# Attention and feed-forward in one kernel: scores in batches of two, the last sum of tiles 0 to 6 turned through DRAM, and tanh operations behind the exps

## The chip, the cores and the metric

One core of a Trainium2 chip runs the whole kernel. The metric is device time in microseconds (us) of one execution: the median of three runs. A core has TensorE (PE, matrix products), ScalarE (ACT), VectorE (DVE), GpSimd (POOL) and SyncE (SP, which only issues transfers here). Each takes its own instructions strictly in order and waits on semaphores for the others.

## What is computed

`x` has 4096 tokens of 256 channels. First attention with 16 heads of 16 channels, then a feed-forward part with three blocks, each inside a layer norm and with a residual:

```
x = x + LN(attention(LN(x)))                   # causal softmax, 16 heads; q, k, v and proj with low-rank terms
x = x + LN(ffn(LN(x)))
ffn: h = x
     for blk in 0, 1, 2:
         y = W[2 blk] h + b;  y = gelu(LN(y) * gamma + beta)
         h = h + W[2 blk + 1] y + b            # six 256 x 256 weights, dequantised, with low-rank terms
```

## The kernel before

A first stage loads and folds weights, projects q, k and v, and writes q and k to DRAM. The rest, which is what the change touches, is `attend_and_feed`. Tokens are cut in 8 tiles of 512. Attention walks through 32 visits (a tile's queries, four heads each). For each block of 128 keys and pair of heads it makes one *score unit*: two products of 64 rows into one of three slots `S` of PSUM (`NS = 3`), then one exp of 128x1024 by ScalarE into `probs`, a ring of twelve. A *weigh* multiplies four heads' `probs` with the values into the one bank `O`: four products on 128x32 strips of the array, of 512 columns each (fewer on the diagonal). At the end of a visit VectorE turns `O`, divides, and SP moves the result to `attT`. There are 1056 score units and 576 weighs.

Meanwhile the *feed* works on tiles whose attention is complete: the output projection, layer norms and the three blocks. Tiles 0 to 6 are fed as 14 halves of 256 tokens in three lanes of buffers, the last tile in four parts after the last exp. A feed *piece* is the product of four strips of 256 columns into the one bank `F`. A half's sum `h` is held with channels on partitions; layer norms want tokens on partitions. In between, a half is turned by a VectorE transpose of 32x32 blocks ("flip"), four transfers to DRAM ("put") and one back ("get"). The last product of the third block, `second2` (called `ENDING`), is made the other way round, with tokens on partitions, so that its result can be normalised where it is; for that TensorE also adds `h` by products with the identity (the branch `c == NC` in the printed function), and `evac_h` on VectorE adds the bias.

What stands where is not decided while it runs. `plan()` walks through the whole stage with durations of its own and writes down an order for each engine; the engines run these orders as they stand. In `plan()`, `next_product` chooses TensorE's next item: a batch of scores goes on while it has fewer than `BATCH` and the next slot is free within `THIRD` us; feed pieces become due at `FEED_FROM + FEED_EACH * tile`; `BACKLOG` is the number of units that weighs may lag. Going over from scores (64 rows) to strips (32 columns) and back is a *turn* below. ScalarE's own list has exps and, for tiles 0 to 6, 42 tanh operations of 128x512 (`gelu0` to `gelu2` of 14 halves), taken ahead of any exp that is ready at the same time.

Of the kernel before, what the change touches and what calls it, by code (L numbers as in the profile page):

```python
# [23 lines left out]
P = 128  # L24
# [9 lines left out]
STRIP = 32  # L34
# [787 lines left out]
FEED_FROM, FEED_EACH = 24.0, 62.0  # L822
BATCH, THIRD, SLACK, BACKLOG = 3, 0.25, 0.5, 10
HOP = 0.15
LANDING = {"k_load": 4.3, "q_load": 4.3, "moved": 1.9, "x_load": 4.2, "store": 3.0, "moved_late": 1.9}
TURNS = ["_x"] + [str(m) for m in range(BLK)]
# [75 lines left out]
def feed_parts():  # L902

    parts = [("evac_att", 0.8, 0.45, ("project",)), ("ln_att", 1.75, 1.05, ("evac_att",)), ("rs_att", 1.9, 1.9, ("ln_att",)),
             ("add_x", 1.5, 1.1, ("rs_att", "x_load")), ("ln_x", 1.75, 1.05, ("add_x",)), ("rs_x", 1.9, 1.9, ("ln_x",)),
             ("norm_x", 0.95, 0.6, ("rs_x",)), ("flip_x", 0.75, 0.0, ("norm_x",)), ("put_x", 2.8, 0.0, ("flip_x",)), ("get_x", 0.7, 0.0, ("put_x",))]
    for m in range(BLK):  # L910
# [38 lines left out]
def plan():  # L949
# [41 lines left out]
    for x in feed:  # L991
# [85 lines left out]
    def next_product(now):  # L1077
# [10 lines left out]
        slack = busy - (now + HOP + us[score] + SWITCH["score"]) if first else 1e9  # L1088
# [21 lines left out]

    locked, F_free, blocked = None, 0.0, {}
# [5 lines left out]
    while len(end) < len(after):  # L1117
# [36 lines left out]
def attend_and_feed(nc, g, d):  # L1154
# [26 lines left out]
    with ExitStack() as ctx:  # L1181
# [124 lines left out]
        with nc.Block() as block:  # L1306

            @block.sync
            def _(sp):
                need = sp.value_load(g["need_max"][0:1, 0:1], min_val=0, max_val=1)  # L1310
                for x in order["SP"]:
# [145 lines left out]
            def _(pe):  # L1457
# [47 lines left out]
                for x in order["PE"]:  # L1505
# [46 lines left out]
                    elif name.startswith("second") and name != ENDING:  # L1552
# [28 lines left out]
            def _(dve):  # L1581
# [64 lines left out]
                for x in order["DVE"]:  # L1646
# [39 lines left out]
                    elif name.startswith("flip"):  # L1686
                        nc.vector.transpose(flat[2][s][:, :], flat[3][s][:, :]).then_inc(dve_ok[s], 1)
# [19 lines left out]
                    elif name.startswith("add") and m is not None:  # L1707
                        for o in range(NC):
                            last = nc.vector.scalar_tensor_tensor(own_t(hT, t, k)[:, o, :], in_channels(name, t, k)[:, o, :],  # L1709
                                                                  g["b2T"][:, m * NC + o:m * NC + o + 1], own_t(hT, t, k)[:, o, :], ALU.add, ALU.add)  # L1710
# [25 lines left out]
                    else:  # L1736
                        link(s, scaled(t, k, own(u, t, k)))
# [55 lines left out]
```

## Time and profile before

| | us |
|---|---|
| median of three runs | 1263.21 (1259.63 to 1264.57) |
| the profiled execution's own time | 1261.49 |
| its span, first to last instruction | 1259.5 |
| PE busy in the span | 1213.4 |
| ACT busy in the span | 1097.8 |
| DVE busy in the span | 754.9 |

Busy time is the union of an engine's instructions. Matmul ends are modelled and two neighbours overlap, so what a product costs is read from the distance between the starts of groups, not from its length. Idle time counts only where the engine is the one that sets the pace.

### The profile page before, as it was taken

To read this page: it belongs to the slowest core of one execution; us is meant where nothing else is said; L and a number is where in the kernel's file an instruction comes from. 1 tells how busy PE (TensorE), PEld (TensorE's weight loads), DVE (VectorE), ACT (ScalarE), POOL (GpSimd) and SP (SyncE) were. 2 spreads that over 40 slices of the span, in tenths; PEclk is the share of its full clock that TensorE was granted. 3 is DMA by queue.
4 is the path that set the end of the run, shared out by engine and by line. 5 is a ranking of instruction groups with operands and counts; after the bars stand their busy time and mean duration, and the time that the engine had idled before them with its cause. 6 is when DMAs were issued, how large, how long until landed. Compare 5 with 4: busy or idle time off the path is not lost.

```text
span 1259.5 us, 30041 instructions
## 1 busy us (share of the span) xinstructions
PE 1213.4 (96%) x11429; PEld 526.9 (42%) x11429; DVE 754.9 (60%) x1820; ACT 1097.8 (87%) x1251; POOL 437.9 (35%) x1373
## 2 busy tenths in 40 slices
PE   8999999999999999999999999999999999999957
PEld 6556434343343433444334334343344333333246
DVE  6775225577765666766665675756666665551066
ACT  4765999999999998999999999999899999999922
POOL 3221235343433552345334253432323431220044
PEclk9999999999999999999999999999999999999989
DMA  5985644644435453454443443543435343331000
GB/s 170 314 307 174 191 122 119 187 150 132 140 102 151 123 143 86 126 164 135 123 122 102 122 119 107 137 118 107 137 86 158 110 129 102 89 93 47 1 5 17
DMA packets 144208, 159.48 MB, mean 127 GB/s; under 512 B 76326, under 2 KB 106044, under 8 KB 144060
## 3 DMA queue, kind: packets, MB, share of 16 engines
q1 hardware_dynamic: 139772, 153.26, 41.0%
q10 hardware_dynamic: 4288, 4.26, 1.1%
q8 instruction: 91, 1.49, 0.5%
q14 instruction: 57, 0.47, 0.1%
HBM read 117.62 MB, written 35.65 MB: 122 GB/s over the span
## 4 chain that ended last, share of the span: by engine, by line
PE 68%; ACT 7%; DVE 5%; issue 3%; DMA 3%; POOL 2%; SPq 2%; ACTq 0%; POOLq 0%; DVEq 0%
PE O L1500 30%; PE S L1482 21%; PE F L209 15%; ACT probs L1425 6%; SPq L595 2%; DMA feed_mem<-turns 2%; DMA qkv_mem<-turns 1%; DVE feed_mem L1703 1%; PE S L1571 1%; DVE feed_mem L1704 1%; DVE o_turned L1652 1%; PE S L1555 0%; POOL rstdC L1385 0%; DVE stC L1594 0%; DVE feed_mem L1727 0%
## 5 line engine op out<-in xcount | busy, mean ns | idle before, releaser
L1425 ACT ACTIVATE probs<-S 128x1024 f32<-128x1024 f32 x1056 | 995.2, 1050 | 65.1 <-PE S L1482 56.1
L1500 PE MATMUL O<-probs,vg 128*32 128x512 f32 (+3 forms) x4608 | 523.9, 564 | 5.3 <-DVE o_turned L1652 3.4
L1482 PE MATMUL S<-q_op,k_op 64*128 64x512 f32 (+3 forms) x2304 | 383.9, 425 | 9.9 <-ACT probs L1425 8.2
L1482 PEld LDWEIGHTS S<-q_op,k_op 64*128 64x128 f32 x2304 | 186.5, 184 | 324.2 <-ACT probs L1425 235.3
L1500 PEld LDWEIGHTS O<-probs,vg 128*32 128x32 f32 x4608 | 120.7, 110 | 208.6 <-issue 177.8
L1403 POOL TENSOR_SCALAR_AFFINE_SELECT probs<-probs 128x512 f32<-128x512 f32 (+1 forms) x160 | 92.9, 590 | 164.6 <-ACT probs L1425 164.0
L1373 POOL TENSOR_SCALAR tmpC<-mvC 128x2 f32<-128x2 f32 x84 | 24.4, 290 | 309.3 <-DVE rstdC L1603 307.4
L209 PE MATMUL F<-wfT,feed_mem 128*32 128x256 f32 x1280 | 83.5, 388 | 3.1 <-DVEq L1637 1.5
L1652 DVE STREAM_TRANSPOSE o_turned<-O 128x512 f32<-128x512 f32 x32 | 22.8, 712 | 97.1 <-PE O L1500 96.1
L1704 DVE SCALAR_TENSOR_TENSOR feed_mem<-feed_mem 128x512 f32<-128x512 f32 x90 | 65.9, 732 | 3.1
L1703 DVE SCALAR_TENSOR_TENSOR feed_mem<-feed_mem 128x512 f32<-128x512 f32 x90 | 63.6, 707 | 3.5 <-DVE qkv_mem L1709 0.5
L1412 POOL TENSOR_TENSOR feed_mem<-feed_mem 128x512 f32<-128x512 f32 x30 | 33.3, 1109 | 91.7 <-DVE feed_mem L1692 91.7
L560 PE MATMUL psQ<-xnT,qkv_mem 128*128 128x512 f32 x128 | 57.1, 599 | 1.7 <-POOL heads_of L449 1.7
L1685 DVE TENSOR_TENSOR feed_mem<-F,bffn 128x512 f32<-128x512 f32 x40 | 27.6, 689 | 50.4 <-PE F L209 50.4
L209 PEld LDWEIGHTS F<-wfT,feed_mem 128*32 128x32 f32 x1280 | 39.2, 111 | 44.3 <-issue 24.9
L1727 DVE TENSOR_SCALAR feed_mem<-feed_mem,rstdC,nmrC 128x256 f32<-128x256 f32 x80 | 34.6, 474 | 36.6 <-POOL nmrC L1384 35.5
L1594 DVE BATCH_NORM_STATS2 stC<-feed_mem 128x6 f32<-128x256 f32 x132 | 49.5, 416 | 10.1 <-DVEq L1637 7.6
L423 ACT ACTIVATE qf<-psQ,cols 128x512 f32<-128x512 f32 x32 | 21.9, 684 | 33.5 <-PE psQ L560 33.5
L1692 DVE TENSOR_SCALAR feed_mem<-feed_mem,halved 128x256 f32<-128x256 f32 x60 | 22.0, 409 | 36.1 <-DMA feed_mem<-turns 36.0
L1385 POOL TENSOR_TENSOR rstdC<-rstdC,minus_half 128x1 f32<-128x1 f32 x24 | 13.3, 554 | 80.2 <-DVE rstdC L1601 80.1
L209 PE MATMUL F<-feed_mem,wfT 128*32 128x256 f32 x640 | 40.9, 382 | 0.0
L560 PEld LDWEIGHTS psQ<-xnT,qkv_mem 128*128 128x128 f32 x128 | 23.7, 190 | 30.2 <-issue 28.3
(210 smaller groups left out, 1254.7 us busy)
## 6 DMA issues: line engine op xcount, KB each, us to landing
k_op<-qk_rows SPq DMA_DIRECT2D x256, 256.0 KB, 3.7
qk_rows<-parts SPq DMA_DIRECT2D x32, 512.0 KB, 4.4
q_op<-qk_rows SPq DMA_DIRECT2D x128, 128.0 KB, 2.9
turns<-feed_mem SPq DMA_DIRECT2D x160, 64.0 KB, 1.9
feed_mem<-turns SPq DMA_DIRECT2D x40, 256.0 KB, 2.9
k_op<-qk_rows SPq DMA_DIRECT2D x48, 128.0 KB, 2.6
x_in<-in_L_attn_x ACTq DMA_DIRECT2D x8, 512.0 KB, 5.3
feed_mem<-in_L_attn_x SPq DMA_DIRECT2D x16, 256.0 KB, 3.5
```

Of the source, the lines that this page charges most:

```text
L209: last = matmul(out[n * STRIP:(n + 1) * STRIP], lhsT[:, n, :] if len(lhsT.shape) == 3 else lhsT[:, n * STRIP:(n + 1) * STRIP], rhs, **how)
L560: last_mm = nc.tensor.matmul(psQ[:, m, :], g["wqkvT"][:, c, m * P:(m + 1) * P], xnT[:, u, c, :], start=(c == 0), stop=(c == NC - 1))
L1403: nc.gpsimd.affine_select(out=tri, in_=tri, compare_op=ALU.is_ge, fill=0.0, base=0, pattern=pattern, channel_multiplier=-1).then_inc(cut_o ...
L1412: nc.gpsimd.tensor_tensor(own_t(uT, t, k), z, z, ALU.mult).then_inc(pool_ok[lane(t, k)], 1)
L1425: nc.scalar.activation(probs[:, n % NP, :, :], S[:, n % NS, :, :], ACT.Exp, scale=SCALE).then_inc(exp_ok, 1)
L1482: last = nc.tensor.matmul(S[:, n % NS, a, at:at + TT - q0], k_op[mine, c % RING, pair, k0:k0 + P], q_op[mine, v % QS, pair, q0:TT], start= ...
L1500: last = nc.tensor.matmul(O[h * STRIP:(h + 1) * STRIP, q0:TT], vg[:, kb, col:col + STRIP], probs[:, n % NP, a, at:at + TT - q0], start=fir ...
L1594: last = nc.vector.bn_stats(st[:, b.start + j, :], src[:, j, :])
L1652: nc.vector.transpose(o_turned[:, :, :].rearrange("p b e -> p (b e)"), O[:, :]).then_inc(o_out, 1)
L1703: link(s, nc.vector.scalar_tensor_tensor(poly, poly, GELU_POLY[n], square, ALU.add, ALU.mult))
L1704: nc.vector.scalar_tensor_tensor(poly, poly, GELU_POLY[n - 1], by, ALU.add, ALU.mult).then_inc(dve_ok[s], 1)
L1727: last = nc.vector.tensor_scalar(flat[3][s].rearrange("p (i b r) -> p b i r", b=nb, r=STRIP)[:, j], src[:, j, :].rearrange("p (i r) -> p i ...
```

## The change

It has three parts, and with new numbers in `plan()` all orders of the stage come out anew. A batch holds at most two scores (`BATCH` 3 to 2, with smaller `THIRD` and `SLACK`), and two waits inside the plan get prices of their own (`SCORE_OUT`, `SLOT_OUT`). A tanh yields to an exp for 4 us after it is ready (`rank_now`). And for tiles 0 to 6 `second2` is made with channels on partitions like the other blocks' second products; `add2` on VectorE adds product, bias and `h` in four operations, and the half is turned by `flip_h`, `put_h` and `get_h` before its last layer norm. The two pieces per half that added `h` on TensorE go. The last tile keeps the old way.

```diff
-FEED_FROM, FEED_EACH = 24.0, 62.0
-BATCH, THIRD, SLACK, BACKLOG = 3, 0.25, 0.5, 10
+FEED_FROM, FEED_EACH = 20.0, 64.0
+BATCH, THIRD, SLACK, BACKLOG = 2, 0.2, 0.1, 11
 HOP = 0.15
+GELU_WAIT = 4.0
+SCORE_OUT, SLOT_OUT = 0.2, 0.15
-TURNS = ["_x"] + [str(m) for m in range(BLK)]
+TURNS = ["_x"] + [str(m) for m in range(BLK)] + ["_h"]
...
-    return 1 if name.startswith("turn") else nb * (NC + 1) if name == ENDING else nb * NC if name[:6] != "second" else NC * NC
+    return 1 if name.startswith("turn") else nb * NC if name[:6] != "second" else NC * NC
...
-    return parts + [("ln_h", 1.75, 1.05, ("evac_h",)), ("rs_h", 1.9, 1.9, ("ln_h",)), ("result", 1.5, 1.1, ("rs_h",)),
+    return parts + [("flip_h", 0.75, 0.0, (f"add{BLK - 1}",)), ("put_h", 2.8, 0.0, ("flip_h",)), ("get_h", 0.7, 0.0, ("put_h",)), ("ln_h", 1.75, 1.05, ("get_h",)), ("rs_h", 1.9, 1.9, ("ln_h",)), ("result", 1.5, 1.1, ("rs_h",)),
...
-        slack = busy - (now + HOP + us[score] + SWITCH["score"]) if first else 1e9
+        slack = busy - (now + SCORE_OUT + us[score] + SWITCH["score"]) if first else 1e9
...
+    def rank_now(x, now):
+
+
+        return 2 if x[0].startswith("gelu") and x[1] < NT - 1 and now < ready["ACT"][x] + GELU_WAIT else rank[x]
...
+                            if x[0] == "put_h":
+                                sp.dma_start(d["turns"][s].rearrange("(b r) (k q) -> r b k q", r=STRIP, q=NC * STRIP)[:, :, i, :],
+                                             flat[3][s][i * STRIP:(i + 1) * STRIP, :].rearrange("r (b q) -> r b q", q=NC * STRIP)).then_inc(put_ok[s], 16)
+                                continue
...
+                        if x[0] == "get_h":
+                            sp.dma_start(u[s], d["turns"][s].rearrange("(b p) n -> p b n", p=P)).then_inc(got_ok[s], 16)
+                            continue
...
-                    elif name.startswith("second") and name != ENDING:
+                    elif name.startswith("second") and (name != ENDING or t < NT - 1):
...
-                        nc.vector.transpose(flat[2][s][:, :], flat[3][s][:, :]).then_inc(dve_ok[s], 1)
+                        into, src = (3, 2) if name == "flip_h" else (2, 3)
+                        nc.vector.transpose(flat[into][s][:, :], flat[src][s][:, :]).then_inc(dve_ok[s], 1)
...
+                            into = flat[2][s].rearrange("p (b i c r) -> p c b i r", b=nb, c=NC, r=STRIP)[:, o]
+                            new, old = (x.rearrange("p (i b r) -> p b i r", b=nb, r=STRIP) for x in (new, old))
+                            for b in range(nb):
+                                last = nc.vector.scalar_tensor_tensor(into[:, b], new[:, b], by, old[:, b], ALU.add, ALU.add)
...
-                        link(s, scaled(t, k, own(u, t, k)))
+                        link(s, scaled(t, k, own(u, t, k), True))
```

How the order of TensorE moves is seen in the middle of the stage. Before, from score unit 477 on (L1482 is a score, two products each; L1500 a weigh, four each; L209 with `wfT` feed pieces, four each, and with `ident` the pieces that add `h`):

```order
L1482 MATMUL S<-q_op,k_op 128x512 x6
L1500 MATMUL O<-probs,vg 32x512 x4
L209 MATMUL F<-wfT,qkv_mem 32x256 x8
L209 MATMUL F<-ident,qkv_mem 32x128 x8
L1482 MATMUL S<-q_op,k_op 128x512 x6
L209 MATMUL F<-wfT,qkv_mem 32x256 x8
L209 MATMUL F<-ident,qkv_mem 32x128 x8
L1500 MATMUL O<-probs,vg 32x512 x4
L1482 MATMUL S<-q_op,k_op 128x512 x6
L1500 MATMUL O<-probs,vg 32x512 x8
L1482 MATMUL S<-q_op,k_op 128x512 x6
L1500 MATMUL O<-probs,vg 32x512 x8
```

With the change, from unit 482 on (the score is now L1499, the weigh L1517):

```order
L1499 MATMUL S<-q_op,k_op 128x512 x4
L1517 MATMUL O<-probs,vg 32x512 x8
L1499 MATMUL S<-q_op,k_op 128x512 x4
L1517 MATMUL O<-probs,vg 32x512 x4
L1499 MATMUL S<-q_op,k_op 128x512 x4
L1517 MATMUL O<-probs,vg 32x512 x8
L1499 MATMUL S<-q_op,k_op 128x512 x4
L1517 MATMUL O<-probs,vg 32x512 x4
L1499 MATMUL S<-q_op,k_op 128x512 x4
L1517 MATMUL O<-probs,vg 32x512 x8
L1499 MATMUL S<-q_op,k_op 128x512 x4
L209 MATMUL F<-qkv_mem,wfT 32x256 x8
```

Three scores and two weighs' worth of strips have become two scores with one and two weighs in turn. Over the whole stage the order has 371 turns there and back before the last score before, and 522 with the change.

On VectorE the end of the attention is the second place. Before (L1685 is `evac_h`, L1594 to L1603 moments, L1621 and L1738 the result, L1652 to L1663 turning and dividing `O`):

```order
L1685 TENSOR_TENSOR feed_mem<-F,bffn 128x512
L1594 BN_STATS stC<-feed_mem 128x6 x2
L1597 BN_AGGR mvC<-stC 128x2 x2
L1602 TENSOR_SCALAR tmpC<-mvC 128x2
L1603 TENSOR_SCALAR rstdC<-tmpC 128x2
L1621 TENSOR_SCALAR feed_mem<-feed_mem,rstdC,nmrC 128x256 x2
L1738 TENSOR_TENSOR feed_mem<-feed_mem 128x512
L1652 STREAM_TRANSPOSE o_turned<-O 128x512
```

With the change (L1741 is `add2`, L1711 the flip, L1611 to L1620 moments, L1675 to L1686 `O`, L1640 and L1769 the result):

```order
L1741 SCALAR_TENSOR_TENSOR feed_mem<-F,cols,feed_mem 128x4x32 x4
L1711 STREAM_TRANSPOSE feed_mem<-feed_mem 128x512
L1611 BN_STATS stC<-feed_mem 128x6 x2
L1614 BN_AGGR mvC<-stC 128x2 x2
L1619 TENSOR_SCALAR tmpC<-mvC 128x2
L1620 TENSOR_SCALAR rstdC<-tmpC 128x2
L1675 STREAM_TRANSPOSE o_turned<-O 128x512
L1680 RECIPROCAL o_rl<-o_turned 128x16
L1682 TENSOR_TENSOR o_turned<-o_turned,o_rl 128x16x16
L1686 STREAM_TRANSPOSE o_div<-o_turned 128x512
L1640 TENSOR_SCALAR feed_mem<-feed_mem,rstdC,nmrC 128x128 x4
L1769 TENSOR_TENSOR feed_mem<-feed_mem 128x512
```

The last half's moments, behind its flip and the transfers, now stand just ahead of the last turning of `O`, and its result behind it; before, the last half was done with one more visit still to come. In TensorE's order its last `second2` piece stands behind score unit 1044 of 1056, where it stood behind unit 985.

## Rows read from the trace of the kernel before

**Rows 1.** The page: busy time of each engine; the last chain by engine.

```profile
PE 1213.4 (96%) x11429; PEld 526.9 (42%) x11429; DVE 754.9 (60%) x1820; ACT 1097.8 (87%) x1251; POOL 437.9 (35%) x1373
PE 68%; ACT 7%; DVE 5%; issue 3%; DMA 3%; POOL 2%; SPq 2%; ACTq 0%; POOLq 0%; DVEq 0%
```

**Rows 2.** Windows: stretch, its length, PE, PEld, DVE, ACT, POOL busy, clock, DMA.

```profile
118.00:1196.00 1078.00, 1058.31 (x10732) 421.48 (x10732) 633.57 (x1436) 1013.48 (x1098) 384.77 (x1210) 1.00 0.42 120
```

**Rows 3.** One line's instructions: the scores (min/median/max ns; first and last start).

```profile
L1482 PE MATMUL S<-q_op,k_op x2304: 215/395/504, 118.0 to 1193.9; 64*128 64x512 f32 x160, 64*128 64x256 f32 x18, 64*128 64x128 f32 x14
```

**Rows 4.** Timeline of PE, 615.96 to 621.78 us, batches of three (start, length).

```profile
615.96 0.97 PE L1482 MATMUL S<-q_op,k_op 64*128 64x512 f32 x6
616.86 1.92 PE L1500 MATMUL O<-probs,vg 128*32 128x512 f32 x16
618.71 1.28 PE L1482 MATMUL S<-q_op,k_op 64*128 64x512 f32 x6
619.92 1.92 PE L1500 MATMUL O<-probs,vg 128*32 128x512 f32 x16
621.78 0.50 PE L1482 MATMUL S<-q_op,k_op 64*128 64x512 f32 x2
```

**Rows 5.** Timeline of PE, 216.34 to 217.99 us, batches of two.

```profile
216.34 0.73 PE L1482 MATMUL S<-q_op,k_op 64*128 64x512 f32 x4
217.00 1.07 PE L1500 MATMUL O<-probs,vg 128*32 128x512 f32 x8
217.99 0.73 PE L1482 MATMUL S<-q_op,k_op 64*128 64x512 f32 x4
```

**Rows 6.** The chain in order of time: two feed pieces.

```profile
591.08 0.86 PE F L209 x16
```

**Rows 7.** Timeline of ACT: exps back to back, and round a tanh (L1435).

```profile
1130.34 65.70 ACT L1425 ACTIVATE probs<-S 128x1024 f32<-128x1024 f32 x71 [0.34 <-PE S L1482]
...
600.87 0.64 ACT L1435 ACTIVATE qkv_mem<-qkv_mem 128x512 f32<-128x512 f32 x1
...
601.39 5.78 ACT L1425 ACTIVATE probs<-S 128x1024 f32<-128x1024 f32 x6
```

**Rows 8.** Timeline of PE, 1157.18 to 1159.02 us: batches of two, one weigh each.

```profile
1157.18 0.91 PE L1482 MATMUL S<-q_op,k_op 64*128 64x512 f32 x4
1158.02 1.07 PE L1500 MATMUL O<-probs,vg 128*32 128x512 f32 x8
1159.02 0.90 PE L1482 MATMUL S<-q_op,k_op 64*128 64x512 f32 x4
```

**Rows 9.** Timelines and a window round two longer stalls of PE.

```profile
484.81 3.60 PE L209 MATMUL F<-wfT,feed_mem 128*32 128x256 f32 x32 [1.54 <-DVEq L1637]
...
486.00:488.00 2.00, 2.00 (x24) 1.04 (x16) 1.90 (x4) 0.00 (x0) 0.00 (x0) 0.50 0.30 107
...
904.77 4.01 PE L1500 MATMUL O<-probs,vg 128*32 128x512 f32 x32 [1.99 <-DVE o_turned L1652]
```

**Rows 10.** Single lines of DVE: additions and flips (min/median/max ns).

```profile
L1709 DVE SCALAR_TENSOR_TENSOR feed_mem<-F,cols,feed_mem x42: 342/477/485, 269.0 to 1229.9; 128x256 f32<-128x256 f32 x40, 128x128 f32<-128x128 f32 x2
...
L1687 DVE STREAM_TRANSPOSE feed_mem<-feed_mem x40: 670/711/714, 206.7 to 1102.8; 128x512 f32<-128x512 f32 x40
```

**Rows 11.** DMA issues (KB, us to landing), one put, SP's waits (total, times, longest).

```profile
turns<-feed_mem SPq DMA_DIRECT2D x160, 64.0 KB, 1.9
feed_mem<-turns SPq DMA_DIRECT2D x40, 256.0 KB, 2.9
...
601.91 2.84 SPq L1343 DMA_DIRECT2D turns<-feed_mem  x4
...
SPq L1319 <- PE S L1482: 220.7, 48, 15.6
```

**Rows 12.** Waits of DVE for a root; timeline of DVE behind the last exp.

```profile
DVE feed_mem L1727 <- POOL nmrC L1384: 35.5, 23, 3.7
...
1203.13 0.43 DVE L1594 BATCH_NORM_STATS2 stC<-S 128x6 f32<-128x256 f32 x1 [3.69 <-PE S L1571]
```

More of the change, by code:

```diff
@@ L910, in feed_parts @@
     for m in range(BLK):
-        out = f"add{m}" if m < BLK - 1 else "evac_h"
         parts += [(f"evac{m}", 0.8, 0.45, (f"first{m}",)), (f"ln{m}", 1.75, 1.05, (f"evac{m}",)), (f"rs{m}", 1.9, 1.9, (f"ln{m}",)),
@@ L915, in feed_parts @@
                   (f"pa{m}", 1.45 + 0.45, 0.0, (f"sq{m}",)), (f"pb{m}", 1.45, 0.0, (f"pa{m}",)), (f"pc{m}", 1.45, 0.0, (f"pb{m}",)),
-                  (f"gate{m}", 0.75, 0.0, (f"gelu{m}",)), (out, 0.9, 0.55, (f"second{m}",))]
-    return parts + [("ln_h", 1.75, 1.05, ("evac_h",)), ("rs_h", 1.9, 1.9, ("ln_h",)), ("result", 1.5, 1.1, ("rs_h",)),
+                  (f"gate{m}", 0.75, 0.0, (f"gelu{m}",)), (f"add{m}", 0.9, 0.55, (f"second{m}",))]
+    return parts + [("flip_h", 0.75, 0.0, (f"add{BLK - 1}",)), ("put_h", 2.8, 0.0, ("flip_h",)), ("get_h", 0.7, 0.0, ("put_h",)), ("ln_h", 1.75, 1.05, ("get_h",)), ("rs_h", 1.9, 1.9, ("ln_h",)), ("result", 1.5, 1.1, ("rs_h",)),
                     ("store", 0.5, 0.5, ("result",))]
@@ L1004, in plan @@
             found += [("moved", 4 * t + i) for i in (0, 1, 2, 3) if n >= 1 + i // 2] + ([("moved_late", 4 * t + 3)] if n >= 2 else [])
-            found += [("exp", NUNIT - 1)] if k else [("evac_h", t - 1, j) for j in range(2)]
+            found += [("exp", NUNIT - 1)] if k else [(f"add{BLK - 1}", t - 1, j) for j in range(2)]
         if n == (lead(name) if t == NT - 1 else 0) and (t < NT - 1 or name != "project"):
@@ L1109, in landing, with hop @@
         return LANDING_FIRST if x[0] == "moved" and x[1] < FIRST_MOVED else LANDING.get(x[0], 0.0)
+    def hop(a, y):
+        return SCORE_OUT if y[0] == "exp" and a[0] == "score" else SLOT_OUT if y[0] == "score" and a[0] == "exp" else HOP
+    def rank_now(x, now):
+        return 2 if x[0].startswith("gelu") and x[1] < NT - 1 and now < ready["ACT"][x] + GELU_WAIT else rank[x]
     locked, F_free, blocked = None, 0.0, {}
@@ L1127, in plan @@
             start = now
-            x = min((x for x, at in ready[e].items() if at <= now), key=lambda x: (rank[x], -left.get(x, 0.0), ready[e][x], str(x)))
+            x = min((x for x, at in ready[e].items() if at <= now), key=lambda x: (rank_now(x, now), -left.get(x, 0.0), ready[e][x], str(x)))
         del ready[e][x]
@@ L1140, in plan @@
             if not waiting[y]:
-                ready[engine[y]][y] = max(end[a] + (0.0 if engine[a] == engine[y] and a[0] not in PUTS else 0.0 if not us[a] else landing(a) if engine[a] == "SP" or a[0] == "moved_late" else HOP) for a in after[y])
+                ready[engine[y]][y] = max(end[a] + (0.0 if engine[a] == engine[y] and a[0] not in PUTS else 0.0 if not us[a] else landing(a) if engine[a] == "SP" or a[0] == "moved_late" else hop(a, y)) for a in after[y])
                 if takes_bank(y):
@@ L1617, in root, with scaled @@
                     return nc.vector.scalar_tensor_tensor(nmr[:, b], mv[:, b, 0], -1.0, r, ALU.mult, ALU.mult)
-                def scaled(t, k, src):
+                def scaled(t, k, src, turned=False):
                     for j, b in enumerate(range(slots(t, k).start, slots(t, k).stop)):
+                        if turned:
+                            for c in range(NC):
+                                last = nc.vector.tensor_scalar(own(y, t, k)[:, j, :].rearrange("p (c k e) -> p c k e", c=NC, e=STRIP)[:, c],
+                                                               src[:, j, :].rearrange("p (k c e) -> p c k e", c=NC, e=STRIP)[:, c],
+                                                               rstd[:, b:b + 1], nmr[:, b:b + 1], ALU.mult, ALU.add)
+                            continue
                         last = nc.vector.tensor_scalar(own(y, t, k)[:, j, :], src[:, j, :], rstd[:, b:b + 1], nmr[:, b:b + 1], ALU.mult, ALU.add)
```

7 lines of the change are left out of this document (5 added, 2 removed).

## The prediction

> **What bounds the kernel now.** I read the page first: PE is busy 96% of the span and carries 68% of the last chain, ACT 87% and 7% [rows 1]. The stage that the change touches runs from the first score unit at 118.0 us to the last at 1193.9 us, 1075.9 us [rows 3]. In it PE is busy 1058 and ACT 1013 of 1078 us, DVE 634 [rows 2]. So two engines are nearly full, and each waits for the other. What PE's busy time hides is found from the starts of groups in its timeline. A batch of two scores takes 0.66 us until the weigh behind it starts, a weigh 0.99 us until the next score [rows 5]; two weighs take 1.85 us and three scores 0.90 us [rows 4]. The differences give 0.86 us for a weigh with 0.13 us on top once for a run of strips, and 0.22 us for a score unit (0.24 by the difference of 0.90 and 0.66; I take 0.22, since 0.66 = 2 x 0.22 + 0.22 and 0.90 = 3 x 0.22 + 0.24) with 0.22 on top once for a batch. One turn there and back so costs 0.35 us. Two feed pieces take 0.86 us [rows 6], so 0.43 each. An exp behind an exp takes 65.70 / 71 = 0.925 us, and a tanh holds the next exp up by 601.39 - 600.87 = 0.52 us [rows 7].
>
> PE's work in the stage: 1056 units x 0.22 = 234 (with three digits 0.222), weighs 453 (480 full ones x 0.858, and 32 of each narrower width, 1.5 x 32 x 0.858), feed pieces 189, and 371 turns x 0.35 = 130. That is 1006 us; PE stands still for the other 70. ACT's work is 1056 x 0.925 + 42 x 0.52 = 999. Neither sum explains 1076 alone. What does is the batch of three with three slots: its third score needs the slot of the unit just ahead of the batch, so PE waits for an exp that ACT can only end when it has nothing more to read. The batch at 615.96 takes 0.90 us, the next, with the same work, 1.21: 0.31 us of standing [rows 4]. If every other one of the 309 batches of three pays that, it is 48 us. Two long stalls are seen besides. At 484.81 PE waited 1.54 us for DVE, and its next four feed pieces took 3.60 in place of 1.72 us, at half the clock (granted share 0.50, so 1.2 GHz, right behind the wait); at 904.77 it waited 1.99 us for the turning of `O`, and four weighs took 4.01 where 3.5 was due [rows 9]. Together about 6 us. Towards the end of the stage, when the feed is through, batches of two with one weigh each come every 1.84 us: that is ACT's pace, and PE stands 0.84 - 0.66 = 0.18 us in each [rows 8]; the order has 28 of them in a row, 5 us. 48 + 6 + 5 leaves 11 us that I can't name.
>
> **The batches.** The order has 522 turns in place of 371: 151 x 0.35 = 53 us of PE work more. In return the third score's wait goes (-48). A batch of two needs slots whose exps ended one exp earlier. So what takes its place? The order gives each cycle (batch and strips behind it) one weigh in 226 cases, 0.35 + 0.44 + 0.86 = 1.65 us, 1.29 us of strips in 142 (2.08 us) and 1.72 in 117 (2.51 us); ACT wants 1.85. By a count 236 cycles are shorter than ACT's and 183 of these stand alone between longer ones. The rows at 216.34 show such a lone short cycle: no wait (0.66) [rows 5]. Those that follow another short one wait 0.18 as at 1157.18 [rows 8]: 236 - 198 (the runs' first ones) = 38, 7 us. It could be nothing if a long cycle ahead has given more play, and 0.18 x 236 = 42 if the lone ones wait as well; I take 7, because rows 5 are that case.
>
> A rule speaks against this part: the Trainium skill, TensorEngine Tiling (Array Packing), Key Properties, has it that a change of tiling mode drains TensorE. The skill's TensorE: Matmul & The Clock Gate puts what a lone matmul can't hide at about 166 ns at full clock. With two drains a turn that is an estimate of 0.33 us and +50 us for 151 turns; the trace's 0.35 agrees, and it has the rest of what a turn costs in it.
>
> **The tanh operations.** Before, one goes ahead of a ready exp, 0.52 us of ACT. Now 29 of 42 stand ahead of the first exp of a batch whose strips before were long (cycle 2.5 us or more, where ACT has 0.65 us free), 13 elsewhere. The first cost nothing, since ACT would wait for the score; the others at most 0.52 - 0.23 = 0.3 us (behind a 2.08 us cycle), together 3 us. A gain beyond that is none: ACT isn't the longer sum.
>
> **The last sum.** For each of 14 halves PE drops two pieces: 28 x 0.43 = -12 us, on the path, since PE has the longest sum. DVE drops `evac_h` (an operation of 128x512 like a flip, about 0.7) and makes four additions of 128x128 (0.34 each, the least of the line that has both forms) and a flip of 0.71 [rows 10], and the result in four operations in place of two, at worst 0.34 x 4 against two of 0.48, the median of a 128x256 there: 1.8 us a half, 25 in all on 634 of 1078, hidden while DVE is ahead of PE. SP issues 4 puts (2.84 us) and a get (0.6): 14 x 3.4 = 48 us of issuing. The half's way to its result grows by 1.4 + 0.7 - 0.7 + 2.8 + 1.9 + 0.6 + 2.9 = 9.6 us [rows 10, 11]. Nothing on PE waits for a result except the next half of the lane, whose place in the order is later by that. It costs nothing as long as DVE isn't held at `ln_h` with PE's inputs behind it; if it is, a case costs what those of rows 9 cost, 2.4 to 3.4 us.
>
> **The end.** The last `second2` piece is now 12 units ahead of the last exp, 11 us. From there addition 1.4, flip 0.7, put 4.7, get 3.5, moments 1.5 (two statistics of 0.43 and four short ones), the root on POOL at most 3.7 (the longest wait of DVE for one), result 2: 17.5 us, so the result ends 6.5 us behind the last exp. The last tile's moments start 7.1 us behind it (1203.13 against 1196.04), after 3.69 us in which DVE is idle, where the result fits [rows 7, 12]. Cost 0; each us beyond 0.6 is one on the time.
>
> **Sum.** PE's work: 1006 + 53 - 12 = 1047. Standing: 7 for short cycles, 3 for tanh, and 6 + 11 = 17 of long and unnamed stalls as before: 27. 1047 + 27 = 1074 against 1076, or -2.3 with the fractions. The profiled execution's own time of 1261.49 becomes 1259.2; it lay 1.7 under the median, so **1260.9** for the median. What is over 0.5%, about 6 us, a measurement of this kernel can tell from no change.
>
> **The rivals.**
> *The stalls go as well (chance 0.35).* The 17 us of long and unnamed standing may come from the same lack of play: a batch of three turns any late exp into a wait, one of two has about one exp of room. Then 10 to 14 us of standing stay in all: 1047 + 12 = 1059, **1246**. For it: the third score's wait is the only stall that repeats in the rows. Against it: rows 9 are stalls on DVE, which the batch doesn't touch.
> *Batches of two wait too (0.16), slower.* ACT's sum of 999 is 95% of PE's 1047, and exps, scores and their semaphores are a loop with a latency of its own. The place is the second score of a batch, the price 0.18 us [rows 8]. The change breaks even at 29 us of standing, 0.056 us a turn; from 35 us on it is slower by over 0.5%, which is reached when 45 more of the 522 batches wait. With one in four, 130 x 0.18 = 23 in place of 7: 1047 + 43 = 1090, **1277**. Against it: rows 5.
> *The new transfers hold DVE up (0.12), slower.* Puts stand in SP's queue behind loads of keys that wait for scores (220.7 us in 48 waits, 4.6 each, at most 15.6) [rows 11]. A get that lands late holds DVE at `ln_h`, and a turning of `O` or a gate behind it stops PE. Five such at 3 us: +15, **1276**; the same at the end of the stage lengthens the time directly.
> *As worked out (0.37):* 1254 to 1269.
>
> **Range and chances.** 1244 to 1280 leaves out the ends: no standing at all (1047, 1234) and all 236 short cycles waiting (+35, 1297). The likeliest case gives 0.30 same, 0.04 faster and 0.03 slower; the first rival 0.33 faster and 0.02 same; the two slow ones 0.25 slower and 0.03 same. Faster 0.37, same 0.35, slower 0.28.
>
> **What would show it.** In PE's timeline batches of two (0.66 us to the next strips) in long rows; nearly none of over 0.75 us except behind a short cycle. PE's starts should add up to 1047 us of work and about 27 of standing between first and last score. ACT's idle time before exps should grow, from 65 us by 20 or so, as PE is now the longer by 48 us. No `second2` identity pieces; the last flip a few us ahead of the last exp. I am wrong if the stage's length moves by more than 10 us, if a turn costs other than 0.35 us, if DVE waits for the new gets with PE behind it, or if the last tile's moments start later than 7.5 us behind the last exp.

## The result, and the profile after

The changed kernel takes 1270.11 us (median, 1267.91 to 1271.62), the kernel before 1262.77 in the same comparison: a ratio of 1.0062, 95% interval 1.0043 to 1.0080. It is slower by 7 us. The forecast of 1260.9 had the wrong sign. Its profiled execution took 1271.02 us, with a span of 1269.3.

The page of the changed kernel, busy time of each engine and the chain that ended last, answers to [rows 1]; the window over the stage to [rows 2].

```profile
PE 1225.4 (97%) x10981; PEld 487.0 (38%) x10981; DVE 771.9 (61%) x1904; ACT 1098.4 (87%) x1251; POOL 435.4 (34%) x1373
...
PE 67%; DVE 6%; SPq 5%; POOL 4%; DMA 4%; ACT 3%; issue 3%; ACTq 0%; DVEq 0%; POOLq 0%
```

```profile
118.00:1204.00 1086.00, 1068.68 (x10281) 380.69 (x10281) 648.30 (x1515) 1013.30 (x1098) 380.68 (x1204) 0.99 0.44 126
```

ACT's work is what it was (1013 us), DVE's grew by 15. PE is busy for 10 us more in this window, which is 8 us longer than that of [rows 2], though 451 products fewer lie in it. The scores of the changed kernel, one line's instructions, answer to [rows 3]:

```profile
L1499 PE MATMUL S<-q_op,k_op x2304: 215/394/792, 117.7 to 1202.4; 64*128 64x512 f32 x160, 64*128 64x256 f32 x18, 64*128 64x128 f32 x14
```

The first score starts at 117.7 us and the last unit at 1202.0 (its last product at 1202.4): the stage is 1084.3 us in place of 1075.9. The rest of the span, ahead and behind, grew by 1.4. The timeline of PE in the middle of it (start, length) answers to [rows 4, 5]:

```profile
484.06 0.73 PE L1499 MATMUL S<-q_op,k_op 64*128 64x512 f32 x4
484.73 1.06 PE L1517 MATMUL O<-probs,vg 128*32 128x512 f32 x8
485.72 0.73 PE L1499 MATMUL S<-q_op,k_op 64*128 64x512 f32 x4
486.38 1.92 PE L1517 MATMUL O<-probs,vg 128*32 128x512 f32 x16
488.24 0.74 PE L1499 MATMUL S<-q_op,k_op 64*128 64x512 f32 x4
488.90 1.07 PE L1517 MATMUL O<-probs,vg 128*32 128x512 f32 x8
```

0.66 us from a batch to its strips, 0.99 and 1.86 from one and two weighs to the next batch: no waits here, and a turn costs the 0.35 us that was reckoned.

**A bookkeeping of PE.** The comparison needs more than such stretches, so I went over the starts of all PE groups between the first and the last score, for each kernel alike. A batch of n scores is due 0.21 + 0.22 n us (0.222 with three digits), a run of strips 0.14 + 0.86 for each weigh's columns; what a group takes over that, until the next one starts, is called waiting here. Unhindered groups fit these dues in all 13 kernels, to 0.02 us for a batch and 0.01 us for a run of strips. Time that PE loses at half its clock is in the waits too, and so are the 0.01 us and 0.02 us by which most batches of two and of three lie over their due (about 6 us of the short waits before, 4 with the change). Then stage = work + 0.35 x turns + waits, and the waits fall in short ones (under 0.5 us) and long ones. "Work" is less where some feed pieces come behind the last score. All in us but turns; the times are medians, those of the kernel before from its first comparison.

| kernel | time | stage | work | turns | short waits | long waits |
|---|---|---|---|---|---|---|
| before | 1262.8 | 1075.9 | 874.5 | 371 | 41.9 | 29.6 |
| changed | 1270.1 | 1084.3 | 861.4 | 522 | 18.9 | 21.3 |
| batches only | 1286.6 | 1102.3 | 874.5 | 523 | 17.4 | 27.4 |
| last sum only | 1258.5 | 1070.4 | 862.5 | 373 | 45.3 | 32.1 |
| tanh rule only | 1260.6 | 1072.0 | 874.5 | 369 | 46.5 | 21.9 |
| all but batches | 1257.4 | 1069.2 | 862.5 | 376 | 44.8 | 30.4 |
| changed, gets at 3.5 | 1264.9 | 1075.5 | 861.6 | 518 | 18.6 | 13.9 |
| all but batches, gets at 3.5 | 1251.9 | 1068.6 | 862.5 | 383 | 49.7 | 22.4 |
| all but batches, slot price | 1268.6 | 1082.9 | 862.5 | 409 | 34.6 | 42.7 |
| both prices | 1249.5 | 1061.5 | 862.5 | 420 | 28.0 | 24.1 |
| changed, no tanh rule | 1267.1 | 1081.5 | 862.5 | 524 | 17.2 | 18.4 |
| before with both prices | 1256.0 | 1068.8 | 874.5 | 416 | 28.2 | 20.4 |
| slot price, gets at 4.0 | 1246.8 | 1059.0 | 862.5 | 421 | 30.9 | 18.3 |

Part of the waits is the clock. By the clock records of the profiled executions, 6.8 us of the stage before ran at a granted 0.50 (1.2 GHz in place of 2.4), 13.7 us with the change, 17.1 us with the slot price alone, and none in "both prices" and "slot price, gets at 4.0". PE loses at most half of such a stretch. The clock also goes with how the executions of one kernel differ: of the 25 of the kernel before that the first four experiments were compared with, the 8 with a mean granted clock of 0.995 or more took 1257.4 to 1262.0 us, the 5 with 0.991 or less 1262.6 to 1265.4.

**Where the long waits come from.** The longest of the changed kernel is at 1058 us. Some names first: `copy` is VectorE's first operation on a half that a get has brought; its operations of 128x512, the polynomials, and a tanh of ACT follow, and the *gate*, on VectorE, makes of them what the next product needs. The *root* is a chain of twelve small GpSimd operations in each layer norm. First SP's timeline, then the chain in order of time. A get is issued behind four loads of keys and lands 5.04 us later:

```profile
1041.80 3.71 SPq L595 DMA_DIRECT2D k_op<-qk_rows  x4
1045.73 0.42 SPq L1365 DMA_DIRECT2D feed_mem<-turns  x1
```

```profile
1045.73 5.04 DMA feed_mem<-turns
1050.76 0.03 issue
...
1051.12 0.41 DVE feed_mem L1716
...
1055.19 0.31 POOL tmpC L1390
...
1061.07 0.21 POOL nmrC L1401
```

Then ACT's and PE's timelines of the same stretch, and PE's windows (length, busy times, granted clock ahead of the two DMA figures):

```profile
1052.62 3.77 ACT L1442 ACTIVATE probs<-S 128x1024 f32<-128x1024 f32 x4 [0.41 <-PE S L1499]
1059.82 0.63 ACT L1452 ACTIVATE feed_mem<-feed_mem 128x512 f32<-128x512 f32 x1 [3.43 <-DVE feed_mem L1728]
...
1057.91 0.50 PE L1499 MATMUL S<-q_op,k_op 64*128 64x512 f32 x2
1061.51 0.79 PE L1499 MATMUL S<-q_op,k_op 64*128 64x512 f32 x2 [3.09 <-ACT probs L1442]
1063.50 2.79 PE L209 MATMUL F<-feed_mem,wfT 128*32 128x256 f32 x24 [1.20 <-DVE feed_mem L1730]
```

```profile
1058.00:1060.00 2.00, 0.42 (x2) 0.10 (x2) 1.72 (x3) 0.18 (x1) 1.76 (x4) 1.00 0.00 0
1060.00:1062.00 2.00, 0.49 (x2) 0.32 (x2) 0.70 (x2) 2.00 (x3) 0.93 (x5) 0.64 0.00 0
...
1064.00:1066.00 2.00, 2.00 (x24) 0.81 (x16) 0.00 (x0) 0.10 (x1) 0.00 (x0) 0.50 0.49 106
```

DVE stood at `copy` (L1716) for the get, its polynomials (L1727, L1728) came late, and ACT stood at a tanh for 3.43 us with ready exps behind it, since it runs its list as it stands. PE's second score waited for the slot of such an exp, 3.09 us; then a gate was late, 1.20 us; and the pieces behind it ran at 0.50 of the clock, 1.2 GHz, at twice their time. In the bookkeeping this chain cost PE 6.7 us: 4.9 until the pieces start, 1.3 in them and 0.5 in the next batch. The late landing isn't all of it. 5.04 us is 1.9 more than the 3.1 that the plan reckoned, and the root in the same chain took 6.1 us (1055.19 to 1061.27) where the plan has 3.1 (`ROOT_POOL`); VectorE waited for it with the gate behind in its list. The tanh didn't need that root: behind the get VectorE's list was worked off without a gap up to its last polynomial. In all, DVE waited 64 us for gets at `copy`, against 46 us before:

```profile
DVE feed_mem L1716 <- DMA feed_mem<-turns: 38.1, 16, 6.2
...
DVE qkv_mem L1716 <- DMA qkv_mem<-turns: 26.0, 10, 9.9
```

Before, the same two rows (at L1692) read:

```profile
DVE feed_mem L1692 <- DMA feed_mem<-turns: 36.0, 16, 8.0
...
DVE qkv_mem L1692 <- DMA qkv_mem<-turns: 9.5, 5, 3.4
```

For the new gets, at the moments of the last layer norm (L1611), it waited another 11 us (8.3 and 2.8).

**The end.** DVE's timeline behind the last exp (which ends at 1204.68) answers to [rows 12]:

```profile
1200.94 0.75 DVE L1611 BATCH_NORM_STATS2 stC<-feed_mem 128x6 f32<-128x256 f32 x2 [5.92 <-DMA feed_mem<-turns]
...
1207.99 1.08 DVE L1640 TENSOR_SCALAR feed_mem<-feed_mem,rstdC,nmrC 128x128 f32<-128x128 f32 x4
1209.11 0.69 DVE L1769 TENSOR_TENSOR feed_mem<-feed_mem 128x512 f32<-128x512 f32 x1
1212.29 0.43 DVE L1611 BATCH_NORM_STATS2 stC<-S 128x6 f32<-128x256 f32 x1 [2.49 <-PE S L1588]
```

The last half's moments waited 5.92 us for its get, and its result is done at 1209.8; there are still 2.49 us to the last tile's moments, which wait for PE. The wait for the get delayed nothing there: the next operation in DVE's list, the last turning of `O`, waited another 3.47 us for PE. The last tile's moments start 7.6 us behind the last exp, against 7.1.

### The profile page after: what moved, and what is told of

Same layout as the page of the kernel before. It is cut to its first block, busy times and chain, and to the rows that moved or that the text cites. A ratio compares the mean times of both kernels' runs of the same rounds, so it can differ in the third digit from the quotient of the medians.

```text
span 1269.3 us, 29300 instructions
## 1 busy us (share of the span) xinstructions
PE 1225.4 (97%) x10981; PEld 487.0 (38%) x10981; DVE 771.9 (61%) x1904; ACT 1098.4 (87%) x1251; POOL 435.4 (34%) x1373
## 4 chain that ended last, share of the span: by engine, by line
PE 67%; DVE 6%; SPq 5%; POOL 4%; DMA 4%; ACT 3%; issue 3%; ACTq 0%; DVEq 0%; POOLq 0%
PE O L1517 30%; PE S L1499 22%; PE F L209 13%; SPq L595 3%; ACT probs L1442 3%; DMA feed_mem<-turns 2%; DMA qkv_mem<-turns 1%; SPq L1357 1%; DVE stC L1611 1%; PE S L1588 1%; SPq L1310 1%; POOL rstdC L1402 0%; PE S L1572 0%; DVE feed_mem L1758 0%; DVE feed_mem L1727 0%
## 5 line engine op out<-in xcount | busy, mean ns | idle before, releaser
L1442 ACT ACTIVATE probs<-S 128x1024 f32<-128x1024 f32 x1056 | 996.8, 1040 | 70.8 <-PE S L1499 52.5
L1517 PE MATMUL O<-probs,vg 128*32 128x512 f32 (+3 forms) x4608 | 543.1, 565 | 4.9 <-DVE o_turned L1675 2.8
L1499 PE MATMUL S<-q_op,k_op 64*128 64x512 f32 (+3 forms) x2304 | 396.7, 427 | 6.2 <-ACT probs L1442 5.0
L1499 PEld LDWEIGHTS S<-q_op,k_op 64*128 64x128 f32 x2304 | 175.1, 185 | 379.3 <-ACT probs L1442 314.6
L1517 PEld LDWEIGHTS O<-probs,vg 128*32 128x32 f32 x4608 | 113.4, 109 | 197.8 <-issue 163.2
L209 PE MATMUL F<-wfT,feed_mem 128*32 128x256 f32 x960 | 64.6, 384 | 3.3 <-DMA feed_mem<-turns 2.1
L1728 DVE SCALAR_TENSOR_TENSOR feed_mem<-feed_mem 128x512 f32<-128x512 f32 x90 | 65.4, 727 | 3.1
L209 PE MATMUL F<-feed_mem,wfT 128*32 128x256 f32 x960 | 65.9, 390 | 1.2 <-DVE feed_mem L1730 1.2
L1727 DVE SCALAR_TENSOR_TENSOR feed_mem<-feed_mem 128x512 f32<-128x512 f32 x90 | 63.6, 707 | 4.7 <-DVE qkv_mem L1708 1.2
L1611 DVE BATCH_NORM_STATS2 stC<-feed_mem 128x6 f32<-128x256 f32 x132 | 49.7, 417 | 18.1 <-DMA feed_mem<-turns 8.3
L1708 DVE TENSOR_TENSOR feed_mem<-F,bffn 128x512 f32<-128x512 f32 x30 | 20.7, 690 | 51.1 <-PE F L209 51.1
L1675 DVE STREAM_TRANSPOSE o_turned<-O 128x512 f32<-128x512 f32 x32 | 22.9, 714 | 47.2 <-PE O L1517 46.6
L423 ACT ACTIVATE qf<-psQ,cols 128x512 f32<-128x512 f32 x32 | 21.9, 684 | 33.5 <-PE psQ L560 33.5
L1716 DVE TENSOR_SCALAR feed_mem<-feed_mem,halved 128x256 f32<-128x256 f32 x60 | 22.0, 409 | 38.8 <-DMA feed_mem<-turns 38.1
L209 PEld LDWEIGHTS F<-feed_mem,wfT 128*32 128x32 f32 x960 | 26.9, 110 | 37.4 <-issue 27.6
L1730 DVE SCALAR_TENSOR_TENSOR feed_mem<-feed_mem 128x512 f32<-128x512 f32 x30 | 20.5, 684 | 33.7 <-ACT feed_mem L1452 32.4
L209 PEld LDWEIGHTS F<-wfT,feed_mem 128*32 128x32 f32 x960 | 26.1, 109 | 37.4 <-issue 24.8
```

Of the source, the lines that this page charges most:

```text
L209: last = matmul(out[n * STRIP:(n + 1) * STRIP], lhsT[:, n, :] if len(lhsT.shape) == 3 else lhsT[:, n * STRIP:(n + 1) * STRIP], rhs, **how)
L1442: nc.scalar.activation(probs[:, n % NP, :, :], S[:, n % NS, :, :], ACT.Exp, scale=SCALE).then_inc(exp_ok, 1)
L1499: last = nc.tensor.matmul(S[:, n % NS, a, at:at + TT - q0], k_op[mine, c % RING, pair, k0:k0 + P], q_op[mine, v % QS, pair, q0:TT], start= ...
L1517: last = nc.tensor.matmul(O[h * STRIP:(h + 1) * STRIP, q0:TT], vg[:, kb, col:col + STRIP], probs[:, n % NP, a, at:at + TT - q0], start=fir ...
L1611: last = nc.vector.bn_stats(st[:, b.start + j, :], src[:, j, :])
L1727: link(s, nc.vector.scalar_tensor_tensor(poly, poly, GELU_POLY[n], square, ALU.add, ALU.mult))
```

## The experiments

Theory A: what decides is the trade of turns against the waits of third scores, and long waits are scattered over any order. Theory B, the rival: the long waits of the changed kernel are made by the transfers of the new last sum. Theory C: the tanh rule makes gates late. Each part was first made alone; the four batch numbers were always changed together, and no run takes `BATCH` apart from `THIRD`, `SLACK` and `BACKLOG`.

### Batches only

```diff
-BATCH, THIRD, SLACK, BACKLOG = 3, 0.25, 0.5, 10
+BATCH, THIRD, SLACK, BACKLOG = 2, 0.2, 0.1, 11
 HOP = 0.15
+SCORE_OUT, SLOT_OUT = 0.2, 0.15
```

(with the two prices used in `plan()` as in the change; the kernel before otherwise)

> The kernel before with the batches part alone (at most two scores, its numbers and two prices in the plan); last sum, tanh rule and feed dates as before. PE work 874 us, 523 turns x 0.35 = 183 us. Theory A (what the change costs is turns against the waits of the third score; long stalls are scattered and come with any new order): waits under 0.5 us fall from 42 to about 20 us, long ones 15 to 30, stage 1092 to 1107 against 1076, time 1279 to 1294. Theory B (the long stalls of the changed kernel come from the new transfers of the last sum): long stalls stay under 10, stage 1085, time about 1272.

1286.58 us, ratio 1.0192 (1.0155 to 1.0229). The stage is 1102.3 us, 26 longer: turns +53 (152 of them), short waits -25, long ones -2. That is Theory A's range. Theory B's is missed: without any new transfer the long waits are 27 us. DVE's waits for the old gets at `copy` (here L1697) are 82 us in place of 46:

```profile
DVE feed_mem L1697 <- DMA feed_mem<-turns: 52.9, 16, 8.0
...
DVE qkv_mem L1697 <- DMA qkv_mem<-turns: 29.0, 9, 5.7
```

PE's long waits didn't grow with them (27.4 against 29.6), so DVE's total for gets doesn't measure what they cost PE.

### Last sum only

The changed kernel with these numbers:

```diff
-FEED_FROM, FEED_EACH = 20.0, 64.0
-BATCH, THIRD, SLACK, BACKLOG = 2, 0.2, 0.1, 11
-GELU_WAIT = 4.0
-SCORE_OUT, SLOT_OUT = 0.2, 0.15
+FEED_FROM, FEED_EACH = 24.0, 62.0
+BATCH, THIRD, SLACK, BACKLOG = 3, 0.25, 0.5, 10
+GELU_WAIT = 0.0
+SCORE_OUT, SLOT_OUT = 0.15, 0.15
```

> The changed kernel with batches of three, their old numbers and the old tanh rule and feed dates: the last sum by flips and DRAM alone. PE work 861 us, 373 turns x 0.35 = 131. Theory A: standing as before, 72 us; stage 1064, time about 1251, 12 us faster. Theory B: the transfers bring 15 us more of long stalls; stage 1079, time about 1266.

1258.51 us, ratio 0.9976 (0.9959 to 0.9993). The 12 us of PE's work are gone (874.5 to 862.5), but waits are 77.4 in place of 71.5, so the stage is 5.5 us shorter, the profiled executions differ by 5.0 (1256.45 against 1261.49), and the medians by 3.1. The median lies halfway between the two theories, the long waits (32.1 against 29.6) nearer to A.

### Tanh rule only

```diff
+GELU_WAIT = 4.0
...
+    def rank_now(x, now):
+
+        return 2 if x[0].startswith("gelu") and x[1] < NT - 1 and now < ready["ACT"][x] + GELU_WAIT else rank[x]
...
-            x = min((x for x, at in ready[e].items() if at <= now), key=lambda x: (rank[x], -left.get(x, 0.0), ready[e][x], str(x)))
+            x = min((x for x, at in ready[e].items() if at <= now), key=lambda x: (rank_now(x, now), -left.get(x, 0.0), ready[e][x], str(x)))
```

> The kernel before with the tanh rule alone. Theory A: 370 turns, nothing but the scatter of a new order, within 5 us of 1263. Theory C (a tanh that yields makes its gate late, and PE waits for the gate): long stalls grow by 10 us or more, time 1273 or more. A gain of 10 us would say that a tanh ahead of an exp was costly.

1260.63 us, ratio 0.9994 (0.9977 to 1.0011): nothing. Long waits are 21.9 in place of 29.6, where Theory C had 10 more. It falls.

### All but the batches

```diff
-BATCH, THIRD, SLACK, BACKLOG = 2, 0.2, 0.1, 11
+BATCH, THIRD, SLACK, BACKLOG = 3, 0.25, 0.5, 10
```

> The changed kernel with the four batch numbers of before (3, 0.25, 0.5, 10), all else as changed. PE work 861, 376 turns x 0.35 = 132. Theory A: standing about 72, stage 1065, time about 1252; the batches then cost 18 us in the changed kernel, whose time is 1270. Theory B: time about 1266, since transfers and not batches carry the loss.

1257.37 us, ratio 0.9964 (0.9945 to 0.9983). So the batches cost 13 us in the changed kernel (1270.1 against 1257.4, of two comparisons): turns +51, short waits -26, long ones -9, work -1, which is +15 in the stage; the two profiled executions differ by 14.1. Theory A had 18, and 1252 us for this kernel's time; it was 5 above that and 9 below Theory B's 1266. Alone they cost 25: turns and short waits are the same in both pairs within 2 us; the long waits are not, and no run says why.

### Gets that are late in the plan too

In the traces of before and changed a get lands 2.5 to 5.7 us after its issue begins, half of them within 3.0 and a quarter after 3.8. The plan reckoned 0.7 + 2.4 = 3.1. Theory L: the long waits come from there. Theory S: from the luck of any order.

```diff
 LANDING.update({x: 2.4 for x in PUTS + GETS})
+LANDING.update({x: 3.5 for x in GETS})
```

In the changed kernel:

> The changed kernel, whose plan reckons 3.5 us in place of 2.4 for the landing of a get (issue 0.7 besides). In the traces a get lands 2.5 to 5.7 us after its issue begins, a quarter of them after 3.8; the plan had 3.1. Theory L (late gets hold VectorE, and make the long stalls of the changed kernel): waits of 0.5 us and more fall from 21 to about 8 us, stage 1072 in place of 1084, time about 1258. Theory S (any order has 20 to 30 us of long stalls, whatever the plan thinks of a get): time 1265 to 1275.

1264.87 us, ratio 1.0024 (1.0011 to 1.0037); 5 us less than the changed kernel. Long waits are 13.9 in place of 21.3, and DVE's waits for gets at `copy` (now L1717) are halved, while those for the new gets, at the moments (L1612), grew:

```profile
DVE feed_mem L1717 <- DMA feed_mem<-turns: 25.2, 11, 7.0
...
DVE stC L1612 <- DMA qkv_mem<-turns: 20.5, 4, 6.0
...
DVE qkv_mem L1717 <- DMA qkv_mem<-turns: 8.1, 5, 4.0
...
DVE stC L1612 <- DMA feed_mem<-turns: 6.5, 2, 5.2
```

At `copy` 33 us against 64, at the moments 27 against 11. The stage at half clock is 3.4 us in place of 13.7, which can be up to 5 of the 7.4 us of long waits. In the kernel with all but the batches:

> Batches of three with the new last sum and the tanh rule, and 3.5 us for a get's landing in the plan. 384 turns. Theory L: long waits fall from 30 to 15 us, time about 1246 against 1257 without. Theory S: 1252 to 1262.

1251.88 us, ratio 0.9914 (0.9898 to 0.9931), 5.5 less than without it. Both go Theory L's way by about half of what it forecast, and both times lie 0.1 us below the fast end of Theory S's range (1265 and 1252). That planning for late gets helps is likely, since both kernels gained 5 us; that it isn't an order's luck is not shown. (This profiled execution took 1256.36 at a mean granted clock of 0.989, the other three 1251.1 to 1252.3 at 0.994, so its row in the table hardly shows the gain.)

### A price for the slot

From an exp's end to the score that takes its slot the plan reckoned 0.15 us. With 0.35 it leaves out third scores that would wait, and makes batches of two or three as they come.

```diff
-SCORE_OUT, SLOT_OUT = 0.2, 0.15
+SCORE_OUT, SLOT_OUT = 0.2, 0.35
```

> Batches of up to three with the new last sum and the tanh rule; the plan reckons 0.35 us in place of 0.15 from an exp's end to the score that takes its slot, so that a third score that would wait is left out more often: 410 turns in place of 376 (+12 us), 227 batches of three in place of 296. Theory A (the waits of third scores are what batches of two take away, and a turn costs 0.35): waits under 0.5 us fall from 45 to about 25 us, so 20 less against 12 more: time about 1250 against 1257. If the short waits don't fall, 1269.

1268.64 us, ratio 1.0046 (1.0032 to 1.0061): a miss. Turns cost 12 us more, as forecast; short waits fell by 10 and not 20; and long waits rose from 30 to 43. The stage at half clock rose from 6.8 to 17.1 us, which can be up to 5 of those 12. The longest wait is again a chain with a late get in it. Its pieces in order of time, and PE's timeline:

```profile
717.77 5.14 DMA qkv_mem<-turns
722.93 0.74 DVE qkv_mem L1716 x2
...
726.05 0.32 POOL tmpC L1390
...
731.91 0.20 POOL nmrC L1401
```

```profile
735.34 1.08 PE L209 MATMUL F<-qkv_mem,wfT 128*32 128x256 f32 x8 [4.01 <-DVE qkv_mem L1730]
```

The get landed 2.0 us after what the plan reckoned; the root (726.05 to 732.11) took 3.0 us more than the plan's 3.1.

Both prices together (with batches of up to three, the new last sum and the tanh rule):

> The two before together: slot price 0.35 and 3.5 us for a get, batches of up to three, 420 turns. Theories A and L: work 862 + turns 147 + standing 25 to 45 = stage 1034 to 1054, time 1228 to 1245 with a last-tile part as in the changed kernel. Theory S: standing 55 or more, 1255 and more.

1249.46 us, ratio 0.9900 (0.9883 to 0.9918): waits of 52 us, above the 25 to 45 that Theories A and L had, and a time 4 us above their range, though below Theory S's. The stage of 1061.5 is 7.5 above their 1054. Here the slot price does what it should: against the kernel with the later gets alone, 37 turns more (+13), short waits 22 less.

### The rest of the accounts

The changed kernel with `GELU_WAIT = 0.0`:

> The changed kernel without its tanh rule. 525 turns. If the rule is worth nothing: 861 + 184 + 40 of standing, time 1265 to 1275. If it is what keeps the short waits of batches of two low, waits under 0.5 us grow from 19 to 30 us and the time to 1281.

1267.05 us, ratio 1.0034 (1.0018 to 1.0050). The rule is worth nothing in batches of two either (without it the median is 3 us less); short waits are 17.2 against 18.9.

The kernel before with both prices in its plan and nothing else:

> The kernel before with the two prices alone in its plan (0.35 us for a slot, 3.5 us for a get), last sum, tanh rule and batch numbers as before. 417 turns. By the bookkeeping: work 874 + turns 146 + standing about 52 as in the kernel with both prices and the new last sum = 1072, time about 1260; so the new last sum is worth about 11 of that kernel's 12 us. If the time is 1252 or less, the prices are, and the last sum is worth little.

1256.02 us, ratio 0.9948 (0.9932 to 0.9965). That is 4 us below the forecast of 1260, with waits of 48.6 in place of 52. The prices alone give half of the gain of both prices with the new last sum; the last sum, the tanh rule and the feed dates together are worth 6.6 us beside them, 12 of work less and some of it given back in waits.

The slot price with 4.0 us for a get:

> As the kernel with both prices, but 4.0 us for a get in place of 3.5. Theory L: a few us less of long stalls, time 1245 to 1249. Theory S (an order's luck): 1244 to 1262 either way.

1246.85 us, ratio 0.9881 (0.9860 to 0.9901), the fastest of all, 1.2% under the kernel before. Long waits are 18.3 in place of 24.1. The time lies in both theories' ranges and doesn't decide between them. Its PE timeline in the middle, where both kinds of batches stand unhindered:

```profile
612.12 0.73 PE L1500 MATMUL S<-q_op,k_op 64*128 64x512 f32 x4
612.79 1.92 PE L1518 MATMUL O<-probs,vg 128*32 128x512 f32 x16
614.64 0.96 PE L1500 MATMUL S<-q_op,k_op 64*128 64x512 f32 x6
615.54 1.92 PE L1518 MATMUL O<-probs,vg 128*32 128x512 f32 x16
617.39 0.73 PE L1500 MATMUL S<-q_op,k_op 64*128 64x512 f32 x4
618.53 1.50 PE L209 MATMUL F<-wfT,feed_mem 128*32 128x256 f32 x24 [0.40 <-DMA feed_mem<-turns]
```

## Why the prediction was wrong

**The bound** was right: PE, with ACT close behind. **PE's work** was right: 1006 + 53 - 12 = 1047 forecast, 861.4 + 522 x 0.35 = 1044 measured. That a turn costs 0.35 us held in every kernel: 53 us for 151 turns. The Trainium skill, TensorEngine Tiling (Array Packing), Key Properties, has it that a change of tiling mode drains TensorE. These runs agree that going over and back costs time; whether the 0.35 us are drains, none of them takes apart.

**The step that failed** is the one on standing: "If every other one of the 309 batches of three pays that, it is 48 us", and then "In return the third score's wait goes (-48)". I took the total of 70 us, gave 48 to a wait that repeats, and only 6 to long stalls, because I had seen two of them. The bookkeeping over all groups says 41.9 us in short waits and 29.6 in long ones. All batches of three together do have 48 us of waits, but 18 of it are long ones, and most of it isn't ahead of the third score. From the second score of a batch to the third it is 0.23 us where nothing waits; what the 309 batches take over that comes to some 19 us, and 86 of them take over 0.1 us more, where I had 154 at 0.31. Another 23 us stand between the third score and the strips, over the 0.32 us where nothing waits. Batches of two took 23 us of short waits away (41.9 to 18.9), not the 43 that my terms come to (48 + 5 + 11 unnamed = 64 before; 7 + 3 + 11 = 21 behind). If the unnamed 11 are counted as short, the 21 behind was well met by 18.9. The long waits were forecast at 6, before and behind, and came to 29.6 and 21.3. So the standing fell from 71.5 to 40 us, by 31 and not by the 43 from 70 to 27: the stage moved by +8.4 us where I had -2.3. At most some 3 us of the difference is the clock (13.7 us of the stage at half clock, 6.8 before).

**The batches.** The trade is +53 against -23 to -26, in both pairs of kernels: a loss of 25 or more before long waits. My sum had it as +53 - 48 + 7 = +12. The slower rival put its extra waits on second scores at 0.18 us; it was not that, since short waits were as low as forecast and nine in ten second scores follow the first by 0.34 us, as where nothing waits.

**The tanh operations.** 3 us of cost reckoned; the runs with and without the rule, in either kind of batch, show no gain of it.

**The last sum.** -12 us of work came exactly (-12.0 alone). The cover that I named for DVE's and SP's work is thinner than I said: alone it gave 3 us in the medians and 5 in the profiled executions, not 12, as waits rose by 6 and the rest of the span by 1. That the new transfers hold DVE up (my third rival) is seen at `ln_h`, the moments of the last norm: 11 us in all, 5.92 of them at the end, where nothing hung on it. Theory B, that they make the long waits, is refuted: batches alone have more long waits than the changed kernel, and more waits of DVE for gets. What lands late is any get, old or new.

**The end.** Reckoned at 0; the last tile's moments began 7.6 us behind the last exp against 7.1. The limit of 7.5 that I gave was passed by a little. I took the root as 3.7 us at most, which was DVE's longest wait for one; the roots themselves take 3.2 to 6.1 us in the trace before. 1.4 us of the loss lie outside the stage, 0.5 of them here; the rest I have not taken apart.

**The other signs.** ACT's idle time ahead of exps was to grow from 65 us by 20 or so. It is 70.8 us, 6 more, and 86.5 us with the batches alone. Of the batches of two 51 took over 0.75 us to their strips, 39 of them behind a short cycle. That 1270.1 lies within 1244 to 1280 is no merit of the sum: its likeliest case ended at 1269, and neither slow rival is what happened.

What stays open is the rest of the long waits: 14 to 18 us are left in the best cases, and each new order throws them anew. Slow roots, which the plan doesn't know, stand beside late gets in both chains shown; no run gave them a price. Kernels that differ in a line of numbers differ by -19 to +12 us in long waits, so the last few us of any of these times belong to an order and not to a rule.

## What to carry to other kernels

Before a wait is credited to a change, sum it over all its occurrences: take the starts of every group of the engine that sets the pace, subtract what the work is due, and sort what is left by size. A repeated short wait and a few long ones look alike in a total, and only the first kind goes with a rule. A static order is as good as the latencies in it: putting a later landing of transfers and a later freed buffer into the plan gave 0.5% on the kernel before (an order's luck not excluded), and 1.2% together with the new last sum, while the batch numbers that were meant to avoid the wait cost 1 to 2%, since their turns cost more than the waits they took away. And where an engine's list has an operation that can be late ahead of work that is ready, a late transfer can stop three engines, as it did at 1058 us.

## What the runs showed of the hardware

A GpSimd operation of two 128x2 tensors takes three times as long while VectorE runs its 128x512 operations with two tensor inputs. In the changed kernel's chain, during them and behind them:

```profile
1056.29 0.66 POOL tmpC L1392
...
1060.20 0.21 POOL tmpC L1398
```

At 1056 DVE had such operations back to back; the last one is this, and then it was idle until 1061.30:

```profile
1059.10 0.69 DVE L1728 SCALAR_TENSOR_TENSOR feed_mem<-feed_mem 128x512 f32<-128x512 f32 x1
```

(L1392 and L1398 are both tensor-tensor operations of the same size.) It holds over the whole trace. Of the 672 such GpSimd operations in the roots of the changed kernel, 56 lie wholly or nearly so under those of VectorE, with a median of 0.65 us; 604 touch none of them, with a median of 0.20 us, and 8 of these take over 0.4 us. That VectorE's operations are the cause is argued from the two lying together, no run took them apart. A whole root so takes 3.2 us at least and 6.1 at most, before and with the change alike; it is on a half's way to its next product.

PE ran at 2.4 GHz until its stop of 3.09 us at 1058; the granted clock fell to 1.2 GHz (0.50) within that stop, the window from 1060 has 0.64, and stayed there through the stop of 1.20 us and the pieces behind it. Three feed pieces took 2.79 us there in place of 1.29.
